# First layer of a four-layer network: twelve pairs of token tiles by seven block products each

## The chip, the cores and the metric

One core of one Trainium2 chip runs the whole program in one launch. The metric is device time in microseconds. TensorE is PE in the profile (its weight loads PEld), VectorE is DVE, ScalarE is ACT, GpSimd is POOL, and SyncE, which here only issues DMAs, is SP.

## The reference, cut to what matters

`x` is 4 x 1024 tokens of 1024 features. The change is in the first of four layers, and in the preparation of the second one's weights, which takes place beside it.

```python
w_masked = L0_attn_weight * elem_mask                    # 1024 x 1024, masked in blocks of 32 x 32
x = layernorm(x + einsum('bsk,nk->bsn', x, w_masked))    # first layer: the whole of it
# second layer, per batch b: weight, bias and a LoRA adapter chosen by b
y = einsum('bsd,od->bso', x, weight) + bias
lo = einsum('bsr,bor->bso', einsum('bsd,brd->bsr', x, A[b]), Bw[b])
x = layernorm(x + y + where(use_lora[b], lo, 0))
# third layer: a sequence model; fourth: a linear layer with routed LoRA experts
```

## The kernel before

The 4096 tokens are 32 tiles of 128, numbered `s` = 0 to 31 in the first layer, 32 to 63 in the second, 64 to 95 in the fourth. Arithmetic is fp32 by splitting: every operand is the sum of a high half (rounded by ACT) and a low half (the rest, by VectorE), and a product of 128 tokens, 128 inputs and 512 outputs is three matmuls, hi by W hi, hi by W lo, lo by W hi (L726 to L728). The identity is added to the weight, so the product already holds `x + x W`. A tile has 8 chunks of inputs (`KC`) and two halves of outputs, 8 x 2 x 3 = 48 matmuls, accumulated in one PSUM bank for each half.

The masked weight `wall_x` is made in the first 43 us: GpSimd multiplies by the mask (L2171), VectorE adds the identity (L1499), ACT takes the high half (L1148), VectorE the low one (L1503). Tiles 0 to 2 run chunk by chunk behind it.

From tile 3 on each tile goes through the same steps. SP loads `x_in` (L504), transposed, into one of two buffers. ACT makes `x_hi` (L1164), VectorE `x_lo` (L1512). TensorE runs `product(s, 0)` and `product(s, 1)`. ACT evacuates each half into `row` (L1169), VectorE takes statistics of each (L1529) and aggregates them (L1534 to L1538), GpSimd takes the root (L2178), ACT makes `shift` (L1176), normalises (L1179) and issues the store (L1182).

Beside tiles 16 to 31 the second layer's weights of batch 0 are made, in 16 parts, one part a tile. SP loads a part (L515); TensorE multiplies the chosen LoRA rows into a bank (`weight_part`, L782); VectorE adds the identity (L1560) and sums bank and part (`weight_sum`, L1562); ACT takes the high half (`weight_hi`, L1236) and VectorE the low one (`weight_lo`, L1568). The rows themselves come from `pick_a` and `pick_b` on TensorE and `take_a`, `take_b` on ACT. In later batches GpSimd makes some of the low halves (L2185).

VectorE also does small tasks once, each beside one tile, in code order: `centre_win` (L1581), `adapter_coef` (L1593), `pick_places`, `mixes`, `take_biases`, `radii`, `first_angle`, nine `angle` (L1656 to L1665), `choose`, `lora_low` (L1626).

Each engine's order in the first layer is plain program order, written out in its own function, and engines meet through counting semaphores. A waiting instruction holds all that is behind it on its engine.

## Time and profile before

| | us |
|---|---|
| median of 3 runs | 1692.5 |
| lowest and highest run | 1691.87, 1694.61 |
| span of the profiled execution | 1690.5 |
| first layer from tile 3 on | about 51 to 376 |

The span is what the trace of one execution covers; the runs are timed from outside and lie about 2 us above it. Busy time of an engine is the sum of what its instructions cover. Matmuls overlap, so that the distance of two starts tells what one costs. In the groups a mean is that of one instruction from start to end. The releaser in brackets is the instruction whose semaphore came last before the idle time ended. The granted clock is the share of TensorE's full clock, of 2.4 GHz, that it was given.

### The profile page before, as it was taken

The numbers are of one execution on the slowest core, as the hardware profiler recorded it, in microseconds if no ns is written. First come the engines' busy times: TensorE is split into PE (matmuls) and PEld (weight loads), VectorE is DVE, ScalarE is ACT, GpSimd is POOL, SyncE is SP. The second block draws the span as 40 slices with busy tenths as digits, with TensorE's granted clock in tenths as the row PEclk, the third lists the DMA queues.
The fourth block names the chain that finished last, engine by engine and source line by source line (L and its number), as shares of the span: only waits on it lengthen the run. The fifth ranks groups of instructions, "written<-read, shape, count | busy, mean of one in ns | idle before, by whom it ended". The sixth has DMA issues, their size and how long they took to land.

```text
span 1690.5 us, 22973 instructions
## 1 busy us (share of the span) xinstructions
PE 1657.1 (98%) x8110; PEld 1341.9 (79%) x8110; DVE 1049.6 (62%) x2004; ACT 648.0 (38%) x939; POOL 434.2 (26%) x371
## 2 busy tenths in 40 slices
PE   8999999999999999999989999999899999999998
PEld 7788888888888888888876666666678788888886
DVE  6444453436555555566777777777967776776633
ACT  3434333433333333322344555555533333433311
POOL 4111111100000000000276777773223221221200
PEclk9999999999999999999999999999999999999999
DMA  7324233333332333332140000002555565555321
GB/s 275 113 100 150 97 116 124 125 112 118 112 110 107 115 113 115 116 138 84 51 171 26 1 1 1 1 1 75 186 179 210 164 204 204 193 190 184 131 88 50
DMA packets 73124, 196.60 MB, mean 116 GB/s; under 512 B 8883, under 2 KB 17075, under 8 KB 72755
## 3 DMA queue, kind: packets, MB, share of 16 engines
q1 hardware_dynamic: 52274, 125.92, 22.3%
q10 hardware_dynamic: 20736, 69.22, 10.2%
q8 instruction: 66, 1.08, 0.3%
q14 instruction: 48, 0.39, 0.1%
HBM read 122.75 MB, written 72.35 MB: 115 GB/s over the span
## 4 chain that ended last, share of the span: by engine, by line
PE 90%; DVE 4%; issue 3%; ACT 1%; POOL 1%; DMA 1%; ACTq 0%; SPq 0%; POOLq 0%; DVEq 0%
PE ps L726 20%; PE ps L728 20%; PE ps L727 20%; PE ps L933 6%; PE ps L875 3%; PE ps L740 3%; PE ps L833 2%; PE ps L881 2%; PE ps L925 2%; PE ps L923 2%; PE ps L924 2%; PE ps L901 1%; PE ps L782 1%; PE ps L847 1%; PE ps L846 1%
## 5 line engine op out<-in xcount | busy, mean ns | idle before, releaser
L726 PE MATMUL ps<-wall_x,x_hi 128*128 128x512 f32 x1008 | 398.8, 396 | 7.6 <-ACT wall_x L1236 3.5
L728 PE MATMUL ps<-wall_x,x_lo 128*128 128x512 f32 x1008 | 393.3, 390 | 0.0
L727 PE MATMUL ps<-wall_x,x_hi 128*128 128x512 f32 x1008 | 393.1, 390 | 0.0
L2178 POOL TENSOR_TENSOR rstd<-var_eps,minus_half 128x1 f32<-128x1 f32 x96 | 78.9, 822 | 882.7 <-DVE minus_mean L1538 882.7
L1529 DVE BATCH_NORM_STATS2 stats<-row 128x6 f32<-128x512 f32 x192 | 133.1, 694 | 175.0 <-ACT row L1169 170.6
L726 PEld LDWEIGHTS ps<-wall_x,x_hi 128*128 128x128 f32 x1008 | 189.5, 188 | 49.4 <-ACT wall_x L1236 5.2
L728 PEld LDWEIGHTS ps<-wall_x,x_lo 128*128 128x128 f32 x1008 | 189.5, 188 | 40.3
L727 PEld LDWEIGHTS ps<-wall_x,x_hi 128*128 128x128 f32 x1008 | 189.8, 188 | 37.2
L726 PE MATMUL ps<-wall_y,x_hi 128*128 128x512 f32 x512 | 202.4, 395 | 0.0
L728 PE MATMUL ps<-wall_y,x_lo 128*128 128x512 f32 x512 | 199.6, 390 | 0.0
L727 PE MATMUL ps<-wall_y,x_hi 128*128 128x512 f32 x512 | 199.4, 389 | 0.0
L1526 DVE TENSOR_TENSOR row<-ps,bias 128x512 f32<-128x512 f32 x128 | 88.0, 687 | 106.2 <-PE ps L728 104.9
L1302 ACT ACTIVATE g<-ps,b 128x512 f32<-128x512 f32 x128 | 83.7, 679 | 122.5 <-PE ps L925 122.0
L933 PE MATMUL ps<-g,w 128*128 128x512 f32 x256 | 125.5, 612 | 0.0
L1164 ACT ACTIVATE x_hi<-ps 128x1024 fp32r<-128x1024 f32 x64 | 65.6, 1025 | 152.2 <-PE ps L740 149.2
L1179 ACT ACTIVATE row<-row,shift,rstd 128x1024 f32<-128x1024 f32 x96 | 119.5, 1244 | 3.2
L728 PEld LDWEIGHTS ps<-wall_y,x_lo 128*128 128x128 f32 x512 | 96.1, 188 | 20.3
L727 PEld LDWEIGHTS ps<-wall_y,x_hi 128*128 128x128 f32 x512 | 96.3, 188 | 19.1
L726 PEld LDWEIGHTS ps<-wall_y,x_hi 128*128 128x128 f32 x512 | 96.2, 188 | 18.7
L1176 ACT ACTIVATE shift<-minus_mean,rstd 128x1 f32<-128x1 f32 x96 | 28.1, 292 | 202.5 <-POOL rstd L2178 202.3
L1562 DVE TENSOR_TENSOR w_first<-ps,w_first 128x512 f32<-128x512 f32 x64 | 44.0, 688 | 87.2 <-PE ps L782 86.7
L1512 DVE TENSOR_TENSOR x_lo<-ps,x_hi 128x1024 fp32r<-128x1024 f32 x64 | 78.0, 1219 | 26.2 <-ACT x_hi L1164 25.9
(282 smaller groups left out, 2827.7 us busy)
## 6 DMA issues: line engine op xcount, KB each, us to landing
x_scratch<-row ACTq DMA_DIRECT2D x64, 512.0 KB, 2.7
x_in<-x_scratch SPq DMA_DIRECT2D x64, 512.0 KB, 3.7
w_first<-in_w_t SPq DMA_DIRECT2D x64, 256.0 KB, 3.0
out<-row ACTq DMA_DIRECT2D x32, 512.0 KB, 2.8
x_in<-in_x_t SPq DMA_DIRECT2D x29, 512.0 KB, 3.4
cx<-x_scratch SPq DMA_DIRECT2D x24, 512.0 KB, 3.9
x_scratch<-cx ACTq DMA_DIRECT2D x24, 512.0 KB, 2.8
w_in<-in_w_t SPq DMA_DIRECT2D x34, 256.0 KB, 3.0
```

What stands on the lines that cost most here:

```text
L726: pe.matmul(bank, hi[:, k], wall[:, k, 0, cols], start=(k == 0), stop=False)
L727: pe.matmul(bank, hi[:, k], wall[:, k, 1, cols], start=False, stop=False)
L728: return pe.matmul(bank, lo[:, k], wall[:, k, 0, cols], start=False, stop=(k == KC - 1))
L740: last = pe.transpose(ps_x[:, k * P:(k + 1) * P], x_in[s % 2][:, k * P:(k + 1) * P], ident[:])
L933: pe.matmul(ps[:, OUT], w2[:, FCH * (n // UNITS) + i], g[:, i], start=(i == 0), stop=(i == FCH - 1)).then_inc(o_done, 1)
L1164: act.activation(flat(x_parts(s)[0]), src, ACT.Identity).then_inc(hi_ready, 1)
L1179: act.activation(row[:, i], row[:, i], ACT.Identity, bias=shift[:, i:i + 1], scale=rstd[:, i:i + 1])\
L1302: act.activation(g[:, i], ps[:, F0 + i % 2], ACT.Silu, bias=of_layer(b1[:, :, i], n))\
L1512: dve.tensor_tensor(lo, src, hi.bitcast(F32), ALU.subtract).then_inc(lo_ready, 1)
L1526: dve.tensor_tensor(row[:, i, cols], ps[:, out_bank(s, half)], bias[:, cols], ALU.add)\
L1529: mark(dve.bn_stats(stats[:, i, half], row[:, i, cols]))
L2178: pool.tensor_tensor(rstd[:, i:i + 1], var_eps[:, i:i + 1], minus_half[:, 0:1], ALU.pow)\
```

## The change

Tiles 5 to 28 are taken in 12 pairs (a, b) = (5, 6), (7, 8), ... A pair is a 2 x 2 block matrix: tile a and tile b by first and last 512 inputs. The weight is 2 x 2 blocks of 512 x 512. The product of the two is made by Strassen's scheme (in Winograd's form) of seven block products in place of eight. The seven left operands are three blocks of the input, A11, A12 (tile a) and A22 (tile b), and four sums of blocks, S1 to S4. The right operands are three blocks of the weight and four sums, T. Each product has 4 chunks x 3 = 12 matmuls, and a pair 84.

- **T** is made once. `t_sums` makes 16 sums of 128x512, in place in the loaded weight, groups 0 and 1 on GpSimd, 2 and 3 on VectorE. `t_hi` on ACT and `t_low` on VectorE split them in eight steps of 128x1024 into `wall_y`, which is free until the second layer's weights.
- **S** is made for every pair by `combine` on GpSimd: four sums of 128x512 into `x_sum`.
- **Splitting**: `op_hi` on ACT and `op_lo` on VectorE, seven each, 128x512.
- **Products**: order A11, A12, S2, S3, S1, S4, A22. A11, S2 and S1 go one on top of the other into bank 0; after each of the three ACT copies the bank into a part of `held` (`hold`), since each partial sum is needed. The other four go into banks 1, 3, 2 and 3, the last on top of the fourth.
- **Joining**: four `join` on VectorE (bank plus held part, into `row`), in place of ACT's four evacuations. Statistics, aggregate, root and normalisation are as before, in another order.
- VectorE's small tasks are in `extra`, called for both tiles of a pair between the low half of S1 and the third join. `split_a` is moved to tile 30, and the buffer `lora_in` holds one half at a time.
- `load_x` of a tile waits for the halves of the pair two tiles back and for the four sums.
- The 16 weight parts are moved beside tiles 29 (6), 30 (5) and 31 (5), with four load buffers in place of two, banks 4 and 6, and the odd low halves on GpSimd. `wall_y` holds T until the last pair's end.
- The semaphore `bias_rows_ready` gives way to a wait of VectorE for its own end, in the last layer.

The core of the diff:

```diff
+S_BEG, S_END = 5, 29
+PAIRS = (S_END - S_BEG) // 2
+PRODUCTS = 7
+A11, A12, S2, S3, S1, S4, A22 = range(PRODUCTS)
+SUM_OF = {S1: 0, S2: 1, S3: 2, S4: 3}
+PLACE_OF = {S2: 0, S3: 1, S4: 2}
+SPREAD_T = ((0, 1), (2, 3), (4, 6), (5, 7))
+GROUPS = 4
+HELD, JOINS, SUMS = 3, 4, 4
+TAIL_PARTS = {S_END: range(0, 6), S_END + 1: range(6, 11), S_END + 2: range(11, PARTS)}
...
+        def op_source(p, j):
+            xa, xb = pair_in(p)
+            if j in SUM_OF:
+                return x_sum[:, SUM_OF[j]]
+            return {A11: xa[:, FIRST_HALF], A12: xa[:, LAST_HALF], A22: xb[:, LAST_HALF]}[j]
+        def op_parts(j):
+            if j in PLACE_OF:
+                return sum_hi[:, PLACE_OF[j]], sum_lo[:, PLACE_OF[j]]
+            slot, first = {A11: (0, 0), A12: (0, GROUPS), S1: (1, 0), A22: (1, GROUPS)}[j]
+            return x_hi[:, slot, first:first + GROUPS], x_lo[:, slot, first:first + GROUPS]
...
+        def op_wall(j, g):
+            if j in (A11, A12, S4):
+                wall, half = wall_x[:, g if j == A11 else GROUPS + g], int(j == S4)
+            else:
+                wall, half = t_place(2 * g + (j in (S2, A22))), int(j in (S2, S3))
+            return [wall[:, i, half * HALF:(half + 1) * HALF] for i in range(2)]
+        def t_sums(eng, semaphore, g, first):
+            b11, b12 = [w0_in[:, g, cols] for cols in (FIRST_HALF, LAST_HALF)]
+            b21, b22 = [w0_in[:, g + GROUPS, cols] for cols in (FIRST_HALF, LAST_HALF)]
+            eng.wait_ge(w0_lo_ready, g + GROUPS + 2)
+            eng.tensor_tensor(b11, b12, b11, ALU.subtract).then_inc(semaphore, 1)
+            eng.tensor_tensor(b12, b22, b12, ALU.subtract).then_inc(semaphore, 1)
+            eng.wait_ge(semaphore, first + 2)
+            eng.tensor_tensor(b22, b22, b11, ALU.subtract).then_inc(semaphore, 1)
+            eng.wait_ge(semaphore, first + 3)
+            eng.tensor_tensor(b21, b21, b22, ALU.subtract).then_inc(semaphore, 1)
...
+                elif paired(s - 2):
+                    p = pair_of(s - 2)
+                    last = A12 if s - 2 == S_BEG + 2 * p else A22
+                    sp.wait_ge(hi_ready, op_count(p, last))
+                    sp.wait_ge(lo_ready, op_count(p, last))
+                    sp.wait_ge(pool_summed, x_sums(p, SUMS - 1))
...
             for s in range(2, A_END):
-                load_x(s + 3)
+                if s != S_END:
...
+                if s == S_END - 2:
+                    for n in range(2):
+                        load_w(n)
+                if s == S_END:
+                    for n in range(2, 6):
+                        load_w(n)
+                    sp.wait_ge(mm_done, product_count(PAIRS - 1, A22))
                     sp.dma_start(a_in[:], a["expert_a"]).then_inc(lora_loaded, 16)
-                if s >= PARTS - 1 and s < 2 * PARTS - 1:
-                    load_w(s - PARTS + 1)
+                    load_x(s + 3)
+                if s > S_END:
+                    for n in TAIL_PARTS[s]:
...
+            def paired_product(p, j):
+                hi, lo = op_parts(j)
+                bank = ps[:, {A11: 0, A12: 1, S2: 0, S3: 3, S1: 0, S4: 2, A22: 3}[j]]
+                pe.wait_ge(hi_ready, op_count(p, j))
+                pe.wait_ge(lo_ready, op_count(p, j))
+                if j == A11:
+                    pe.wait_ge(evac_act, held_count(p - 1, 2) if p > 0 else evac_count(S_BEG - 2, 0))
+                elif j == A12 and p == 0:
+                    pe.wait_ge(evac_act, evac_count(S_BEG - 2, 1))
+                elif j == A12:
+                    pe.wait_ge(evac_dve, join_count(p - 1, 0))
+                elif j == S2:
+                    pe.wait_ge(evac_act, held_count(p, 0))
+                elif j == S3 and p == 0:
+                    pe.wait_ge(evac_act, evac_count(S_BEG - 1, 1))
+                elif j == S3:
+                    pe.wait_ge(evac_dve, join_count(p - 1, 3))
+                elif j == S1:
+                    pe.wait_ge(evac_act, held_count(p, 1))
+                elif j == S4 and p > 0:
+                    pe.wait_ge(evac_dve, join_count(p - 1, 2))
+                elif j == A22:
+                    pe.wait_ge(evac_dve, join_count(p, 1))
+                opens = j not in (S2, S1, A22)
+                for g in range(GROUPS):
+                    if p == 0 and j == S2:
+                        pe.wait_ge(w0_hi_ready, t_count(2 * g + 1))
+                        pe.wait_ge(w0_lo_ready, t_count(2 * g + 1))
+                    w_hi, w_lo = op_wall(j, g)
+                    pe.matmul(bank, hi[:, g], w_hi, start=(opens and g == 0), stop=False, skip_group_check=not opens)
+                    pe.matmul(bank, hi[:, g], w_lo, start=False, stop=False, skip_group_check=not opens)
+                    last = pe.matmul(bank, lo[:, g], w_hi, start=False, stop=(g == GROUPS - 1),
+                                     skip_group_check=not opens)
+                last.then_inc(mm_done, 1)
...
+            for s in range(FIRST, S_BEG):
+                product(s, 0)
+                product(s, 1)
+            for p in range(PAIRS):
+                for j in range(PRODUCTS):
+                    paired_product(p, j)
+                    if p == pair_of(8) and j == S1:
+                        first_biases()
+                    if p == PAIRS - 1 and j in (A12, S3):
+                        pick_b(0, int(j == S3))
+                    if p == PAIRS - 1 and j == S4:
+                        pick_a(0)
+            for s in range(S_END, A_END):
                 if s == A_END - 1:
                     turn_x(A_END)
-                if s >= PARTS and s % 2 == 0:
-                    pick_a((s - PARTS) // 2)
-                product(s, 0)
-                if s == PARTS - 1:
-                    pick_b(0, 0)
-                if s >= PARTS:
-                    weight_part(s - PARTS)
-                product(s, 1)
-                if s == PARTS - 1:
-                    pick_b(0, 1)
-                if s == 8:
-                    first_biases()
+                for i in range(PARTS // 2):
+                    half, k = i // 4, i % 4 * 2
+                    product(s, half, range(k, k + 2))
+                    if i < len(TAIL_PARTS[s]):
+                        n = TAIL_PARTS[s][i]
+                        if n % 2 == 0 and n // 2 + 1 < KC:
+                            pick_a(n // 2 + 1)
+                        weight_part(n)
...
+            def hold(p, i):
+                act.wait_ge(mm_done, product_count(p, (A11, S2, S1)[i]))
+                if p > 0:
+                    act.wait_ge(evac_dve, join_count(p - 1, (0, 3, 2)[i]))
+                act.activation(held[:, i], ps[:, 0], ACT.Identity).then_inc(evac_act, 1)
...
+            for p in range(PAIRS):
+                a, more = S_BEG + 2 * p, p + 1 < PAIRS
+                if p > 0:
+                    op_hi(p, A22)
+                hold(p, 0)
+                if more:
+                    op_hi(p + 1, A11)
+                normalise(a - 1)
+                if more:
+                    op_hi(p + 1, A12)
+                else:
+                    split_x(S_END)
+                hold(p, 1)
+                if more:
+                    op_hi(p + 1, S2)
+                    op_hi(p + 1, S3)
+                else:
+                    take_b(0, 0)
+                hold(p, 2)
+                if more:
+                    op_hi(p + 1, S1)
+                else:
+                    take_b(0, 1)
+                extra(a)
+                extra(a + 1)
+                if more:
+                    op_hi(p + 1, S4)
+                normalise(a)
...
+            def join(p, i):
+                a = S_BEG + 2 * p
+                s, half, bank, part = ((a, 0, 1, 0), (a + 1, 1, 3, 2), (a, 1, 2, 2), (a + 1, 0, 3, 1))[i]
+                cols = slice(half * HALF, (half + 1) * HALF)
+                dve.wait_ge(mm_done, product_count(p, (A12, S3, S4, A22)[i]))
+                dve.wait_ge(evac_act, held_count(p, part))
+                dve.wait_ge(stored[s % 2], 16 * (s // 2))
+                dve.tensor_tensor(row[:, s % 2, cols], ps[:, bank], held[:, part], ALU.add).then_inc(evac_dve, 1)
...
+            for g in range(2, GROUPS):
+                t_sums(dve, summed, g, KC + 1 + SUMS * (g - 2))
+            split_x(FIRST)
+            half_stats(0, 0)
+            half_stats(0, 1)
...
+            for p in range(PAIRS):
+                a, more = S_BEG + 2 * p, p + 1 < PAIRS
+                if p > 0:
+                    join(p - 1, 3)
+                    op_lo(p, A22)
+                    joined_stats(p - 1, 3)
+                    aggregate(a - 1)
+                if more:
+                    op_lo(p + 1, A11)
+                join(p, 0)
+                joined_stats(p, 0)
+                if more:
+                    op_lo(p + 1, A12)
+                    op_lo(p + 1, S2)
+                    op_lo(p + 1, S3)
+                else:
+                    split_x(S_END)
+                join(p, 1)
+                joined_stats(p, 1)
+                if more:
+                    op_lo(p + 1, S1)
+                extra(a)
+                extra(a + 1)
+                join(p, 2)
+                joined_stats(p, 2)
+                aggregate(a)
+                if more:
+                    op_lo(p + 1, S4)
...
+            def combine(p):
+                xa, xb = pair_in(p)
+                for s in range(S_BEG + 2 * p, S_BEG + 2 * p + 2):
+                    pool.wait_ge(x_loaded[s % 2], 16 * x_loads(s))
+                if p > 0:
+                    pool.wait_ge(lo_ready, op_count(p - 1, S1))
+                pool.tensor_tensor(x_sum[:, 0], xb[:, FIRST_HALF], xb[:, LAST_HALF], ALU.add).then_inc(pool_summed, 1)
+                pool.wait_ge(pool_summed, x_sums(p, 0))
+                pool.tensor_tensor(x_sum[:, 1], x_sum[:, 0], xa[:, FIRST_HALF], ALU.subtract).then_inc(pool_summed, 1)
+                pool.tensor_tensor(x_sum[:, 2], xa[:, FIRST_HALF], xb[:, FIRST_HALF], ALU.subtract).then_inc(pool_summed, 1)
+                if p > 0:
+                    pool.wait_ge(lo_ready, op_count(p - 1, S4))
+                pool.wait_ge(pool_summed, x_sums(p, 1))
+                pool.tensor_tensor(x_sum[:, 3], xa[:, LAST_HALF], x_sum[:, 1], ALU.subtract).then_inc(pool_summed, 1)
```

How the instructions stand now on three of the engines. On VectorE at the start, behind the last mask, before: `w0_in` is the masked weight that is loaded, `wall_x` its halves.

```order
L1503 TENSOR_TENSOR wall_x_106<-w0_in_109,wall_x_106 128x1024
L1499 TENSOR_TENSOR w0_in_109<-w0_in_109,ident_51 128x128
L1503 TENSOR_TENSOR wall_x_106<-w0_in_109,wall_x_106 128x1024
L1512 TENSOR_TENSOR x_lo_128<-x_in1_126,x_hi_127 128x1024
L1529 BN_STATS stats_74<-row_129 128x6 x2
```

And after (L542 to L547 are `t_sums`, L1786 is the low half of tile 3):

```order
L1773 TENSOR_TENSOR wall_x_106<-w0_in_109,wall_x_106 128x1024
L1769 TENSOR_TENSOR w0_in_109<-w0_in_109,ident_51 128x128
L1773 TENSOR_TENSOR wall_x_106<-w0_in_109,wall_x_106 128x1024
L542 TENSOR_TENSOR w0_in_109<-w0_in_109 128x512
L543 TENSOR_TENSOR w0_in_109<-w0_in_109 128x512
L545 TENSOR_TENSOR w0_in_109<-w0_in_109 128x512
L547 TENSOR_TENSOR w0_in_109<-w0_in_109 128x512
L542 TENSOR_TENSOR w0_in_109<-w0_in_109 128x512
L543 TENSOR_TENSOR w0_in_109<-w0_in_109 128x512
L545 TENSOR_TENSOR w0_in_109<-w0_in_109 128x512
L547 TENSOR_TENSOR w0_in_109<-w0_in_109 128x512
L1786 TENSOR_TENSOR x_lo_128<-x_in1_126,x_hi_127 128x1024
```

Eight sums have moved in ahead of the low half of tile 3.

On VectorE in the middle of the layer, one tile before, with a small task (`angle`, its first steps) behind the statistics of a half:

```order
L1529 BN_STATS stats_74<-row_129 128x6
L1534 BN_AGGR mean_var_75<-stats_74 128x2
L1537 TENSOR_SCALAR var_eps_76<-mean_var_75 128x1
L1538 TENSOR_SCALAR minus_mean_77<-mean_var_75 128x1
L1512 TENSOR_TENSOR x_lo_128<-x_in1_126,x_hi_127 128x1024
L1529 BN_STATS stats_74<-row_129 128x6
L1560 TENSOR_TENSOR w_first_166<-w_first_166,ident_51 128x128
L1562 TENSOR_TENSOR w_first_166<-ps,w_first_166 128x512
L1568 TENSOR_TENSOR wall_y_107<-w_first_166,wall_y_107 128x512
L1656 TENSOR_TENSOR sq_re_54<-anchor_53 128x4
```

And a piece of a pair after: L1825 is `join`, L1831 statistics, L1810 `op_lo`, L1958 the first step of an angle.

```order
L1825 TENSOR_TENSOR row_129<-ps,held_185 128x512
L1831 BN_STATS stats_74<-row_129 128x6
L1810 TENSOR_TENSOR x_lo_128<-x_in1_126,x_hi_127 128x512
L1810 TENSOR_TENSOR sum_lo_184<-x_sum_182,sum_hi_183 128x512 x2
L1825 TENSOR_TENSOR row_129<-ps,held_185 128x512
L1831 BN_STATS stats_74<-row_129 128x6
L1810 TENSOR_TENSOR x_lo_128<-x_sum_182,x_hi_127 128x512
L1958 TENSOR_TENSOR sq_re_54<-anchor_53 128x4
L1959 TENSOR_TENSOR sq_im_55<-anchor_53 128x4
```

The small task stands between two joins of one pair now, not at a tile's end.

On SP's queue at the end of the layer before, loads of a tile and of a weight part in turn:

```order
L504 DMA x_in0_125<-in_x_t 128x1024
L515 DMA w_first_166<-in_w1_t 128x512
L504 DMA x_in1_126<-in_x_t 128x1024
L515 DMA w_first_166<-in_w1_t 128x512
L495 DMA x_in0_125<-x1_scratch 128x1024
L515 DMA w_first_166<-in_w1_t 128x512
```

And after (L618 loads a tile of the second layer, L642 a weight part, L731 the matrix `a_in` of the last layer's experts):

```order
L642 DMA w_more_167<-in_w1_t 128x512 x2
L642 DMA w_first_166<-in_w1_t 128x512 x2
L731 DMA a_in_154<-in_expert_a 128x1024
L618 DMA x_in0_125<-x1_scratch 128x1024
L618 DMA x_in1_126<-x1_scratch 128x1024
L642 DMA w_more_167<-in_w1_t 128x512 x2
L642 DMA w_first_166<-in_w1_t 128x512 x2
L642 DMA w_more_167<-in_w1_t 128x512
```

The loads of tiles 32 and 33 stand ahead of those of parts 6 to 10.

## Rows read from the trace of the kernel before

**Rows 1.** The page: busy time and instructions of each engine over the span.

```profile
PE 1657.1 (98%) x8110; PEld 1341.9 (79%) x8110; DVE 1049.6 (62%) x2004; ACT 648.0 (38%) x939; POOL 434.2 (26%) x371
```

**Rows 2.** Windows: the first layer from tile 3 on, and a place far behind.

```profile
core 0: us, PE busy (x) PEld busy (x) DVE busy (x) ACT busy (x) POOL busy (x), PEclk, DMA share, GB/s
52.00:376.00 324.00, 322.22 (x1432) 266.44 (x1432) 135.80 (x372) 127.40 (x183) 44.26 (x32) 1.00 0.34 120
...
863.00:867.00 4.00, 1.86 (x11) 1.33 (x11) 4.00 (x3) 0.61 (x1) 2.62 (x2) 1.00 0.55 168
867.00:870.00 3.00, 2.00 (x9) 2.01 (x10) 2.83 (x6) 1.20 (x2) 1.91 (x1) 0.52 0.89 325
```

**Rows 3.** Timeline of TensorE in tile 16: start, duration, line, what.

```profile
195.17 0.39 PE L726 MATMUL ps<-wall_x,x_hi 128*128 128x512 f32 x1
...
199.72 0.39 PE L728 MATMUL ps<-wall_x,x_lo 128*128 128x512 f32 x1
```

**Rows 4.** Timeline of GpSimd and VectorE beside the first tiles; idle time and releaser in brackets.

```profile
29.51 1.92 POOL L2171 TENSOR_TENSOR w_in<-w_in,block_on 128x1024 f32<-128x1024 f32 x1 [1.46 <-DVE block_on L1493]
...
37.58 1.23 DVE L1503 TENSOR_TENSOR wall_x<-w_in,wall_x 128x1024 fp32r<-128x1024 f32 x1
37.61 2.97 POOL L2171 TENSOR_TENSOR w_in<-w_in,block_on 128x1024 f32<-128x1024 f32 x1 [2.44 <-DVE block_on L1493]
...
40.68 0.29 DVE L1499 TENSOR_TENSOR w_in<-w_in,ident 128x128 f32<-128x128 f32 x1 [1.88 <-POOL w_in L2171]
```

**Rows 5.** Groups of instructions from 52 to 376 us: busy, mean ns, idle before.

```profile
L2178 POOL TENSOR_TENSOR rstd<-var_eps,minus_half 128x1 f32<-128x1 f32 x31 | 43.2, 1395 | 275.8 <-DVE minus_mean L1538 275.8
L1529 DVE BATCH_NORM_STATS2 stats<-row 128x6 f32<-128x512 f32 x62 | 42.8, 694 | 170.6 <-ACT row L1169 170.6
L1179 ACT ACTIVATE row<-row,shift,rstd 128x1024 f32<-128x1024 f32 x31 | 38.6, 1244 | 1.0
L1169 ACT ACTIVATE row<-ps 128x512 f32<-128x512 f32 x60 | 35.8, 598 | 118.7 <-PE ps L728 113.2 <-DMA x_scratch<-row 2.7 <-ACT row L1179 2.7
...
L1568 DVE TENSOR_TENSOR wall_y<-w_first,wall_y 128x512 fp32r<-128x512 f32 x16 | 11.1, 692 | 11.2 <-ACT wall_y L1236 11.2
L1562 DVE TENSOR_TENSOR w_first<-ps,w_first 128x512 f32<-128x512 f32 x16 | 10.9, 683 | 0.3
L1236 ACT ACTIVATE wall_y<-w_first 128x512 fp32r<-128x512 f32 x16 | 10.1, 632 | 24.2 <-DVE w_first L1562 24.2
...
L1534 DVE BATCH_NORM_AGGREGATE mean_var<-stats 128x2 f32<-128x12 f32 x31 | 6.5, 209 | 1.1
...
L1626 DVE SCALAR_TENSOR_TENSOR lora<-lora_in,low_row,lora 128x1024 fp32r<-128x1024 f32 x2 | 2.5, 1268 | 0.0
```

**Rows 6.** Groups of GpSimd over the whole span.

```profile
L2178 POOL TENSOR_TENSOR rstd<-var_eps,minus_half 128x1 f32<-128x1 f32 x96 | 78.9, 822 | 882.7 <-DVE minus_mean L1538 882.7
...
L2185 POOL TENSOR_TENSOR wall_x<-w_more,wall_x 128x512 fp32r<-128x512 f32 x8 | 10.3, 1292 | 23.0 <-ACT wall_x L1236 23.0
```

**Rows 7.** Timeline: TensorE at tiles 3 and 4, and the issue of a store.

```profile
50.87 0.44 PE L726 MATMUL ps<-wall_x,x_hi 128*128 128x512 f32 x1
...
59.50 0.33 ACTq L1182 DMA_DIRECT2D x_scratch<-row  x1
...
62.98 0.47 PE L726 MATMUL ps<-wall_x,x_hi 128*128 128x512 f32 x1 [1.01 <-issue]
```

**Rows 8.** Timeline of VectorE: first step of the adapter coefficients; one angle, first and last.

```profile
91.78 0.29 DVE L1593 TENSOR_REDUCE group<-ident 128x3 f32<-128x48 f32 x2
...
203.69 0.15 DVE L1656 TENSOR_TENSOR sq_re<-anchor 128x4 f32<-128x4 f32 x1
...
204.97 0.16 DVE L1665 TENSOR_TENSOR anchor<-anchor,fix 128x4 f32<-128x4 f32 x1
```

**Rows 9.** The page's DMA issues: count, size, median us from issue to landing.

```profile
w_first<-in_w_t SPq DMA_DIRECT2D x64, 256.0 KB, 3.0
...
x_in<-in_x_t SPq DMA_DIRECT2D x29, 512.0 KB, 3.4
```

398 lines of the change are left out of this document (283 added, 115 removed).

## The prediction

> **What bounds the kernel now.** I read the busy table first: TensorE is busy 98% of the span, VectorE 62%, GpSimd 26% [rows 1]. Then the windows: in the whole stretch that the change rewrites, 52 to 376 us, TensorE is busy 322.2 of 324 us at a granted clock of 1.00, with VectorE at 136 us and GpSimd at 44 [rows 2]. So the first layer is bound by the number of matmuls alone; what the other engines do there is hidden, and their time counts only where the new order makes TensorE wait for it. The price of a matmul is its spacing, not its duration: from the one at 195.17 to the twentieth after it at 199.72 are 4.55 us, 0.2275 us each (both are listed as 0.39, since they overlap) [rows 3].
>
> **What is saved.** A pair of tiles took 2 x 48 = 96 matmuls and takes 7 x 12 = 84; 12 pairs save 144. 144 x 0.2275 = **-32.8 us**. The 16 products for the next weights and the picks are moved, not removed. All further terms are waits that TensorE gets in exchange. One product of twelve lasts 2.73 us, a pair 19.1.
>
> **What is added at the start.** Sixteen 128x512 sums of first-layer weights (T) stand on GpSimd (8) and on VectorE (8), the latter ahead of tile 3's low half. GpSimd and VectorE disturb each other there today: GpSimd's mask takes 1.92 us, but 2.97 when it starts just behind VectorE's 1024-wide subtraction of 1.23 us [rows 4], so that subtraction keeps the other out for 2.97 - 1.92 = 1.05 us, 0.18 less than it is listed with. A 128x512 operation on two SBUF operands is listed with 1.29 us on GpSimd and 0.69 on VectorE [rows 5, 6]; I take 1.07 to 1.1 and 0.55 for what each holds. The last mask ends at 37.61 + 2.97 = 40.58. Today VectorE's next step starts right then [rows 4]; now GpSimd goes straight on with its first sum to 41.9. VectorE's last identity ends at 42.1, its last low half falls behind GpSimd's third sum and ends at 45.5; then the five GpSimd sums that are left and the first five of VectorE alternate, 5 x (1.07 + 0.55) = 8.1, to 53.6; VectorE's other three, each of which needs the one before, take 2.1, to 55.7; the low half of tile 3 takes 1.2 and ends at 56.9. TensorE began tile 3 at 50.87 [rows 7]: +6.1. The 1.0 to 1.2 us that it waits today ahead of tile 4, for that tile's low half (to 62.98), goes, as ACT and VectorE are then ahead: **+4.9** (between 2, if the two engines do not exclude each other for these shapes, and 9, if every sum is stretched as the mask was).
>
> The Trainium skill ("SBUF — State Buffer", section on the two separate sides) has the rule behind this: GpSimd and a VectorE operation with two SBUF inputs take a shared pair of ports for a whole instruction each, while one that reads PSUM with one SBUF operand is outside the rule. The trace agrees: GpSimd's root takes 1.40 us on average in the first layer, where low halves read two SBUF operands, and (78.9 - 43.2) / 65 = 0.55 in the later layers, where they read PSUM [rows 5, 6]. By the rule the new joins (PSUM plus held) cost nothing beside GpSimd; without it they would add up to 4 x 0.5 us to a pair.
>
> **The first wait inside the pairs.** TensorE's third product of a pair goes to the bank of its first and so waits until ACT has copied that one into held. For pair 0 that copy stands far back in ACT's row. Let T be the end of tile 4's last matmul. The first four halves of pair 0 need the buffers of tile 3, and ACT and VectorE, kept busy by T, reach them late; only behind their four low halves, by my count at T+0.5, does VectorE take the second statistics of tile 3. These and the aggregate take it to T+1.6, GpSimd's root to T+3.2, shift and normalise on ACT to T+4.8. Then ACT issues the store (0.45), evacuates (0.5), makes two 1024-wide high halves of T (2.0), evacuates (0.5), makes three high halves (1.6) and copies (0.6) [rows 5, 7]: T+10.4. TensorE is there after two products, T+5.5: **+4.9** (3 to 8).
>
> **The pairs' own circle.** A tile's buffer is loaded again only when both halves of the pair's last operand and the four sums have been read. Around that circle, TensorE apart: landing 3.4 [rows 9]; three dependent GpSimd sums, 3 x 1.29 plus 0.35 of exclusion, 4.2; high half 0.6 and low half 0.7 with 0.8 of exclusion, 2.1; join, statistics, low half of S1, 2.0; next join, statistics, aggregate, 1.85; root 1.0, shift 0.3, normalise 1.24, store issue 0.45, 3.0; high and low half of A22, 1.3 [rows 5, 6]. With 0.35 for handovers this is 18.2 us, against 19.1 of TensorE: a margin of only 0.9 us. But VectorE's other work of the first layer (`extra`) stands inside this circle, between the low half of S1 and the join after S4, where today it lies in VectorE's idle time. By pair: centring 2.8 (two 1024-wide steps and two small ones) and adapter coefficients 1.9 (from 91.78 on) = 4.7; places and mixes 2.2; bias, low half of the window and nine small ones 2.5; eleven small ones 1.6; two angles (203.69 to 205.13 = 1.44 each), one LoRA half 1.27 and a choice 0.3 = 4.5; two angles 2.9; two and a LoRA half 4.2; two 2.9; one 1.4 [rows 5, 8]. Together 26.9, estimates where no row stands (small ones at 0.15). What exceeds the margin in these nine pairs is 26.9 - 9 x 0.9 = **+18.8**; pairs 9 to 11 have none. The bounds are 6 and 27: circle 2.6 us shorter than TensorE's pair, or as long.
>
> The joins, the held copies and the seven halves of a pair otherwise fit: ACT has 7 x 0.63 + 3 x 0.6 + 2 x 1.99 = 10.2 us of 19.1, VectorE about 11.5 and GpSimd about 7.5. If the circle above were not there, these would cost nothing.
>
> **The tail.** All 16 weight parts are now beside tiles 29 to 31, 6, 5 and 5, every 1.4 us of matmuls, where they were one per 11 us. The first pick waits for ACT about 0.9. Parts 6 to 10 are queued on SP behind the load for tile 33, which waits for the low half of tile 31, that is for the end of tile 29 plus 2.3 us; with two issues (0.8), landing 3.5, identity 0.3 and sum 0.7 part 6 is summed about 8 us after tile 29's end, and TensorE needs it for part 8 after 4.8: +3.4 [rows 5, 9]. A chunk of A behind the normalisation of tile 29 on ACT costs 2.2, one of 0.5, and the last choice, now after the sums, 1.3. Sum **+8.5** (3 to 12, the bounds being only the queue, and all of it with slower landings). The later load of tile 33 itself is hidden by the 20 us that follow.
>
> **The clock.** Around 865 TensorE is busy 1.86 of 4 us, and the next 3 us are granted 0.52 [rows 2], the 1.2 GHz level. The new waits of 4 to 6 us at the start could do the same; most of what runs slowly there is followed by another wait, which takes it up. **+1.5** (0 to 8).
>
> **Sum.** -32.8 + 4.9 + 4.9 + 18.8 + 8.5 + 1.5 = +5.8 on the profiled 1690.5, a span of 1696.3. The median of the runs, 1692.5, lies 2.0 above that span, so 1698.3; I say **1698**. A measurement tells 0.2%, 3.4 us: faster is below 1689.1, slower above 1695.9.
>
> **Rivals.**
> 1. Near: the circle lasts 17.5, not 18.2, with 3.0 us for a landing as the weights have [rows 9] and no exclusion. The margin is 1.6; the extras' excess is 12.7, the tail 7, the clock 0.5: -32.8 + 9.8 + 12.7 + 7 + 0.5 = -2.8, 1689.7 (this case reaches to 1693). For it: landings of 3.0 are common in the page. Against: each sum on GpSimd meets two-operand work on VectorE.
> 2. Clearly faster (other side): the circle lasts at most 16.5, because handovers and roots cost what they do undisturbed (0.55). The extras' excess falls to 6.2, start and pair 0 to 6 together, tail 5, clock nothing: -15.6, **1677**. The point that decides is a circle of 17.5 us, a margin of 1.6: there the excess is 12.7, about the 32.8 - 9.8 - 8.5 - 1.5 = 13.0 that start and tail leave of the saving. Against it are the exclusions of [rows 4].
> 3. Dearer: exclusion and landings at full price. The circle is as long as TensorE's pair, extras cost 27, start 12, tail 11, clock 5: +22, **1714.5**.
> 4. The change does not do what it says, for instance since waits of its own keep the pairs in the old time: 1692.5.
>
> **How the numbers follow.** Forecast case (1693 to 1704) 0.46, near 0.25, clearly faster 0.17, dearer 0.10, no effect 0.02. Slower by over 0.2%: 0.40 of the forecast case and 0.10 of the dearer one, 0.50. Within 0.2%: 0.06 + 0.18 + 0.02 = 0.26. Faster: 0.17 + 0.07 = 0.24. The range 1683 to 1709 leaves out most of 2 and 3, 0.2 in all.
>
> **What would show it.** In the changed profile: 144 matmuls fewer; tile 3 of TensorE starting near 57; about 5 us of idle TensorE ahead of the first S2, released by ACT's held; in pairs 0 to 8 idle time ahead of S2 of about extras less 0.9 (3.8 in pair 0, 0.5 in pair 8) and none in pairs 9 to 11; 3.4 us ahead of part 8; the granted clock below 1 after the start's waits. The prediction is wrong if pairs with extras run at 19.1 us (then rival 2), if also pairs without them take more (then rival 3, the circle alone is too long), or if the wait is named for a row's join or a load instead of the held copy.

## The result, and the profile after

| | us |
|---|---|
| median of 4 runs of the changed kernel | 1704.7 |
| lowest and highest | 1703.9, 1708.7 |
| median of 4 runs of the kernel before, same chip | 1693.4 |
| ratio of the runs | 1.0071, 95% interval 1.0059 to 1.0083 |
| profiled span after (before 1690.5) | 1703.5 |

The changed kernel is slower by 11.3 us, 0.7%. The forecast was 1698, slower by 5.5, with a range to 1709. The busy table of the changed kernel's page:

```profile
PE 1642.0 (96%) x7966; PEld 1321.5 (78%) x7966; DVE 1147.5 (67%) x2120; ACT 672.3 (39%) x995; POOL 517.8 (30%) x435
```

Against [rows 1] TensorE has 144 matmuls fewer, VectorE 98 us more to do and GpSimd 84. Where the time went is seen at one landmark, ACT's normalisation of tile 31, the last of the first layer. The timeline of ACT, before (first fence) and after:

```profile
380.30 1.24 ACT L1179 ACTIVATE row<-row,shift,rstd 128x1024 f32<-128x1024 f32 x1
...
852.13 1.24 ACT L1179 ACTIVATE row<-row,shift,rstd 128x1024 f32<-128x1024 f32 x1
```

```profile
391.64 1.24 ACT L1402 ACTIVATE row<-row,shift,rstd 128x1024 f32<-128x1024 f32 x1
...
865.37 1.24 ACT L1402 ACTIVATE row<-row,shift,rstd 128x1024 f32<-128x1024 f32 x1
```

The first layer ends 11.3 us later; the second rows, of the second layer's last tile, are 13.2 apart, so that 1.9 more came in the second layer, which the change leaves alone; later layers add nothing. The windows of the changed kernel (columns as in [rows 2]): the first layer, two pieces of it, and the piece of the second layer that lost the 1.9.

```profile
52.00:386.00 334.00, 303.39 (x1284) 244.05 (x1284) 229.70 (x486) 149.05 (x237) 114.13 (x88) 0.97 0.32 117
57.50:61.50 4.00, 4.00 (x10) 3.11 (x10) 3.86 (x11) 1.53 (x2) 1.89 (x2) 0.50 0.61 202
113.50:116.50 3.00, 3.00 (x8) 2.32 (x7) 2.46 (x7) 1.23 (x2) 1.09 (x2) 0.50 0.53 175
...
775.50:779.00 3.50, 3.50 (x10) 2.71 (x9) 1.93 (x3) 1.54 (x2) 0.07 (x1) 0.51 0.42 164
```

Where [rows 2] had 1.8 us of idle TensorE in 324, there are 30.6 in 334, and stretches at a granted clock of 0.50, the 1.2 GHz level. Three more of them are at 199, 243 and 359 us. The waits themselves, in TensorE's timeline (idle time and releaser in brackets): tile 3, the first S2, those of pairs 1 and 5, weight part 8.

```profile
56.71 0.77 PE L865 MATMUL ps<-wall_x,x_hi 128*128 128x512 f32 x1 [6.15 <-issue]
...
88.42 0.47 PE L946 MATMUL ps<-wall_y,sum_hi 128*128 128x512 f32 x1 [1.68 <-ACT x_hi L1370]
...
112.94 0.47 PE L946 MATMUL ps<-wall_y,sum_hi 128*128 128x512 f32 x1 [3.72 <-ACT held L1377]
...
198.17 0.47 PE L946 MATMUL ps<-wall_y,sum_hi 128*128 128x512 f32 x1 [3.09 <-ACT held L1377]
...
359.57 0.77 PE L962 MATMUL ps<-b_rows,a_rows 128*128 128x512 f32 x1 [4.26 <-DVE w_more L1864]
```

The profile puts the first S2 down to a high half that ran beside ACT's copy; the copy itself ended at 88.21, 0.2 us before S2 starts.

At the start the sums of T are held off as forecast. Timeline of GpSimd and VectorE there:

```profile
46.67 1.74 POOL L542 TENSOR_TENSOR w_in<-w_in 128x512 f32<-128x512 f32 x1
48.37 1.74 POOL L543 TENSOR_TENSOR w_in<-w_in 128x512 f32<-128x512 f32 x1
...
47.29 1.67 DVE L545 TENSOR_TENSOR w_in<-w_in 128x512 f32<-128x512 f32 x1
48.99 1.67 DVE L547 TENSOR_TENSOR w_in<-w_in 128x512 f32<-128x512 f32 x1
...
54.05 0.69 DVE L545 TENSOR_TENSOR w_in<-w_in 128x512 f32<-128x512 f32 x1
55.39 1.22 DVE L1786 TENSOR_TENSOR x_lo<-x_in,x_hi 128x1024 fp32r<-128x1024 f32 x1
```

Each engine starts a sum every 1.7 us while the other works too; with GpSimd done, VectorE's takes 0.69. Tile 3's low half ends at 56.6, and TensorE goes on.

Below, a wait is the distance of two matmul starts less the usual 0.2275. By that measure the waits ahead of S2 in pairs 1 to 9 are 3.9, 0.3, 1.7, 1.0, 3.3, 1.2, 3.2, 1.2 and 0.4, together 16.1. S2 of pair p + 1 stands behind the small tasks that are called in pair p.

### The profile page after: what moved, and what is told of

Its sections match the earlier page's. It is cut to its first block, busy times and chain, and to the rows that moved or that the text cites. A ratio compares the mean times of both kernels' runs of the same rounds, so it can differ in the third digit from the quotient of the medians.

```text
span 1703.5 us, 23156 instructions
## 1 busy us (share of the span) xinstructions
PE 1642.0 (96%) x7966; PEld 1321.5 (78%) x7966; DVE 1147.5 (67%) x2120; ACT 672.3 (39%) x995; POOL 517.8 (30%) x435
## 4 chain that ended last, share of the span: by engine, by line
PE 76%; DVE 9%; issue 5%; ACT 4%; POOL 3%; DMA 2%; ACTq 0%; SPq 0%; POOLq 0%; DVEq 0%
PE ps L865 13%; PE ps L867 13%; PE ps L866 13%; PE ps L1113 6%; PE ps L1055 3%; PE ps L879 3%; PE ps L946 2%; PE ps L948 2%; PE ps L947 2%; PE ps L1061 2%; PE ps L1013 2%; PE ps L1104 2%; PE ps L1105 2%; PE ps L1103 2%; ACT row L1402 1%
## 5 line engine op out<-in xcount | busy, mean ns | idle before, releaser
L2558 POOL TENSOR_TENSOR rstd<-var_eps,minus_half 128x1 f32<-128x1 f32 x96 | 66.4, 692 | 761.4 <-DVE minus_mean L1840 748.7
L865 PE MATMUL ps<-wall_x,x_hi 128*128 128x512 f32 x624 | 251.1, 402 | 12.8 <-issue 6.1
L867 PE MATMUL ps<-wall_x,x_lo 128*128 128x512 f32 x624 | 245.9, 394 | 0.0
L866 PE MATMUL ps<-wall_x,x_hi 128*128 128x512 f32 x624 | 245.7, 394 | 0.0
L865 PEld LDWEIGHTS ps<-wall_x,x_hi 128*128 128x128 f32 x624 | 118.8, 190 | 40.0 <-issue 10.2
L867 PEld LDWEIGHTS ps<-wall_x,x_lo 128*128 128x128 f32 x624 | 118.6, 190 | 25.7
L866 PEld LDWEIGHTS ps<-wall_x,x_hi 128*128 128x128 f32 x624 | 119.0, 191 | 23.1
L1803 DVE BATCH_NORM_STATS2 stats<-row 128x6 f32<-128x512 f32 x144 | 99.8, 694 | 17.3 <-ACT row L1392 12.9
L866 PEld LDWEIGHTS ps<-wall_y,x_hi 128*128 128x128 f32 x512 | 96.2, 188 | 19.1
L1864 DVE TENSOR_TENSOR w_first<-ps,w_first 128x512 f32<-128x512 f32 x56 | 38.5, 689 | 88.3 <-PE ps L962 87.5
L1786 DVE TENSOR_TENSOR x_lo<-ps,x_hi 128x1024 fp32r<-128x1024 f32 x64 | 78.0, 1219 | 27.0 <-ACT x_hi L1356 26.6
```

Of the source, the lines that this page charges most:

```text
L865: pe.matmul(bank, hi[:, k], wall[:, k, 0, cols], start=(k == 0), stop=False)
L866: pe.matmul(bank, hi[:, k], wall[:, k, 1, cols], start=False, stop=False)
L867: return pe.matmul(bank, lo[:, k], wall[:, k, 0, cols], start=False, stop=(k == KC - 1))
L1786: dve.tensor_tensor(lo, src, hi.bitcast(F32), ALU.subtract).then_inc(lo_ready, 1)
L1803: mark(dve.bn_stats(stats[:, i, half], row[:, i, cols]))
L2558: pool.tensor_tensor(rstd[:, i:i + 1], var_eps[:, i:i + 1], minus_half[:, 0:1], ALU.pow)\
```

## The experiments

All ran beside the kernel before on their own chip (medians 1692.9 to 1693.2). Each edits the changed kernel; times are to be held against its 1704.7.

**e1: the small tasks behind the chain.** On VectorE, and on ACT:

```diff
                 if more:
                     op_lo(p + 1, S1)
-                extra(a)
-                extra(a + 1)
                 join(p, 2)
                 joined_stats(p, 2)
                 aggregate(a)
                 if more:
                     op_lo(p + 1, S4)
+                extra(a)
+                extra(a + 1)
...
-                extra(a)
-                extra(a + 1)
                 if more:
                     op_hi(p + 1, S4)
                 normalise(a)
+                extra(a)
+                extra(a + 1)
```

> Change undone in one part only: VectorE's small tasks (extra) come after the aggregate and the low half of S4, so behind the chain that leads to the held copy (ACT's part of extra moves behind the pair's last normalisation). Theory (the small tasks delay join, aggregate, root, normalisation and so the held copy, on which S2 waits, and the waits of over 3 us drop the clock for 3.4 us each): the waits ahead of S2 in pairs 1 to 9, 16 us in the changed kernel, fall to under 3, and the three slow stretches at 113, 199 and 243 us go: 1704.7 - 13 - 5 = 1687. Rival 1 (the pair's circle itself is too long, VectorE late wherever the tasks stand): 1702 to 1705. Rival 2 (the slow clock costs nothing, as another wait takes it up): 1691 to 1692.

Measured 1689.7, ratio to before 0.9977 (0.9967 to 0.9988). Of TensorE's groups from 92 to 300 us, the one with the most idle time ahead of it, in the changed kernel (one more, `x_hi`, has 1.2) and in e1:

```profile
L946 PE MATMUL ps<-wall_y,sum_hi 128*128 128x512 f32 x75 | 31.8, 424 | 14.6 <-ACT held L1377 14.5
```

```profile
L946 PE MATMUL ps<-wall_y,x_hi 128*128 128x512 f32 x88 | 35.1, 399 | 4.2 <-ACT held L1377 4.2
```

S2 (`sum_hi`) waits no more; S1 (`x_hi` by T), which needs the second copy, waits 4.7 in three pairs. The first layer ends 16.8 us sooner. Rival 1 falls. The three slow stretches in the pairs were to go, and there are still four in all, at 54, 88, 194 and 341 us, with as much slow time as in the changed kernel. The time lies between the theory's 1687 and rival 2's 1691. So the gain is of waits, and the clock's part is not told by this run.

**e2: VectorE's sums behind the low halves.**

```diff
-            for g in range(2, GROUPS):
-                t_sums(dve, summed, g, KC + 1 + SUMS * (g - 2))
             split_x(FIRST)
             half_stats(0, 0)
             half_stats(0, 1)
             aggregate(0)
+            t_sums(dve, summed, 2, KC + 1)
             split_x(FIRST + 1)
+            t_sums(dve, summed, 3, KC + 1 + SUMS)
```

> VectorE's eight sums for T come behind the low halves of tile 3 (four) and tile 4 (four) in place of ahead of tile 3's. Theory (ACT's list before pair 0 is what ends last): tile 3 starts near 51.5 in place of 56.7, and the slow stretch at 55 to 62 us goes, but the held copy of pair 0 comes no more than 1 us sooner, so that the wait ahead of the first S2 grows from 1.8 to 6 or more: 1703 to 1704. Rival (start and pair 0 add up, as the prediction summed them): 5.2 of wait and 3.4 of slow clock less, 1696.

Measured 1705.8, 1.0073 (1.0055 to 1.0091). Tile 3 starts at 51.3, and the time comes back ahead of pair 0's first and third product:

```profile
76.28 0.47 PE L946 MATMUL ps<-wall_x,x_hi 128*128 128x512 f32 x1 [2.97 <-DVE x_lo L1810]
...
87.98 0.76 PE L946 MATMUL ps<-wall_y,sum_hi 128*128 128x512 f32 x1 [4.38 <-ACT x_hi L1370]
```

The two terms of the start are not independent: what is spared at tile 3 is waited for at pair 0.

**e3: tile 33's load behind those of parts 6 to 10.**

```diff
-                if s != S_END:
+                if s != S_END and s != S_END + 1:
                     load_x(s + 3)
...
                 if s > S_END:
                     for n in TAIL_PARTS[s]:
                         load_w(n)
+                if s == S_END + 1:
+                    load_x(s + 3)
```

> The load of tile 33 is queued on SP behind the loads of weight parts 6 to 10, not ahead. Theory (those loads stand behind one that waits for tile 31's low half): the wait of 4.25 us ahead of part 8's product goes, and with it the slow stretch at 359 to 362.5 us (1.7): 1699. Rival (the next wait, for a chunk of A, takes its place): 1703 to 1705.

Measured 1699.7, 1.0043 (1.0024 to 1.0063): 5 us, as the theory had it. Part 8 no longer waits; the wait for a chunk of A behind it grows only from 1.0 to 1.7. Groups of TensorE from 336 to 392 us, changed kernel and e3:

```profile
L962 PE MATMUL ps<-b_rows,a_rows 128*128 128x512 f32 x16 | 7.0, 440 | 5.4 <-DVE w_more L1864 5.4
```

```profile
L964 PE MATMUL ps<-b_rows,a_rows 128*128 128x512 f32 x17 | 7.1, 418 | 1.1 <-DVE w_more L1866 1.1
```

**e4: the three together,** and on ACT before pair 0:

```diff
             t_hi(5)
-            normalise(3)
             evacuate(4, 0)
             t_hi(6)
             t_hi(7)
             evacuate(4, 1)
+            normalise(3)
```

> The three together, and on ACT tile 3's normalisation behind both evacuations of tile 4 in place of ahead of the first. Theory (all terms of the sum but about 3.5 us at pair 0 and 5 in the tail are waits that the order makes; nearly no slow stretches in the first layer): 32.8 saved, some 15 us of waits left, 1.7 of clock: 1675 to 1678. Rival (waits replace each other, the pairs are bound by VectorE and GpSimd): 1688 or more.

Measured 1682.1, 0.9928 (0.9910 to 0.9946). Faster than both, 4 us above the upper end of the expectation: the first layer ends 12.2 us before that of the kernel before, with some 18 us of waits and 3.2 of slow matmuls, and 3.5 are given back in the second layer at a slow stretch near 750.

**e5: the waits filled with small matmuls,** so that the clock stays up.

```diff
                 for j in range(PRODUCTS):
+                    keep_busy(7, {(1, 2): 15, (5, 2): 12, (7, 2): 12, (0, 2): 6, (3, 2): 5, (2, 2): 0, (6, 2): 3, (8, 2): 3}.get((p, j), 0))
                     paired_product(p, j)
...
             for s in range(FIRST, S_BEG):
+                if s == FIRST:
+                    keep_busy(7, 25)
                 product(s, 0)
...
+                        keep_busy(5, {8: 14}.get(n, 0))
                         weight_part(n)
```

> The changed kernel with small matmuls put on TensorE, into a bank that nobody reads, ahead of the products that it waits for (25 ahead of tile 3, 15 ahead of pair 1's S2, 12 at pairs 5 and 7, 14 at weight part 8, a few at others), each stretch of them shorter than the wait that it fills. Theory (the slow clock behind a long wait is a cost of its own, about 7.8 us of slow matmuls in the first layer): no slow stretch there, no product started later, 1704.7 - 7 = 1698, somewhat less if the next wait grows. Rival (the slow matmuls are paid out of later waits): the waits left grow by as much, 1703 to 1705.

Measured 1704.4, 1.0067 (1.0053 to 1.0081): the rival. The same windows as above are at full clock:

```profile
57.50:61.50 4.00, 4.00 (x19) 3.30 (x19) 3.90 (x10) 1.54 (x2) 2.27 (x2) 1.00 0.67 214
113.50:116.50 3.00, 3.00 (x15) 2.47 (x14) 2.29 (x6) 1.43 (x2) 1.16 (x2) 1.00 0.55 175
```

Slow matmuls, counted as what their distances have above 0.2275 us, cost 3.3 us in place of 8.9, and yet the first layer ends only 0.1 sooner. The 2.6 us of the stretch at 55 had been taken out of pair 0's wait: S2 now waits 3.1 behind its filler and 4.6 with it, not 1.8. The same holds in part for the pairs: filler and wait ahead of S2 in pairs 1 to 9 are 18.1 us here, where the waits were 16.1. The three slow stretches in the pairs, 4.8 us, give 2.2 back; the normalisation of tile 28 stands 2.4 sooner, 0.2 of it from the start. The tail, where a chunk of A then waits 3.1 in place of 1.0 and the clock falls behind that wait, gives these away again.

**e6: GpSimd's sums of T on 4 columns.**

```diff
             for g in range(2):
-                t_sums(pool, pool_summed, g, SUMS * g)
+                pool.wait_ge(w0_lo_ready, g + GROUPS + 2)
+                for i in range(SUMS):
+                    w = w0_in[:, g + GROUPS * (i // 2), HALF * (i % 2):HALF * (i % 2) + 4]
+                    at_least(pool, pool_summed, SUMS * g + i)
+                    pool.tensor_tensor(w, w, w, ALU.add).then_inc(pool_summed, 1)
```

> GpSimd's eight sums for T are made on 4 columns in place of 512, so groups 0 and 1 of T are left out; VectorE still makes its eight ahead of tile 3's low half. Theory (VectorE is held off by GpSimd, not busy: its sums are listed with 1.7 us beside GpSimd's, 0.69 alone): all eight take 0.7 us each, tile 3 starts within 1 us of the kernel before (51 in place of 56.7) and pair 0 keeps its own wait ahead of S2 of about 5: 5 us and the slow stretch at 55 us less, 1697 to 1699. Rival (eight sums on VectorE cost their own time): tile 3 near 56 still, 1703 to 1705.

The kernel leaves out half of T, so its results are not those of the network; it is there for its time. Measured 1699.0, 1.0044 (1.0029 to 1.0060); the profiled execution took 1704.0. On VectorE:

```profile
42.80 0.68 DVE L542 TENSOR_TENSOR w_in<-w_in 128x512 f32<-128x512 f32 x1
...
47.50 0.69 DVE L547 TENSOR_TENSOR w_in<-w_in 128x512 f32<-128x512 f32 x1
49.06 1.23 DVE L1786 TENSOR_TENSOR x_lo<-x_in,x_hi 128x1024 fp32r<-128x1024 f32 x1 [0.87 <-ACT x_hi L1356]
```

All eight fit into the time that VectorE idles away before tile 3's high half. Tile 3 starts at 50.42, with no wait. So the 6.3 us at tile 3 are the exclusion, not the work. Pair 0's wait is 4.8 here.

**e7: the input sums on 4 columns,** from the second pair on:

```diff
+                n = HALF if p == 0 else 4
+                FH, LH = slice(0, n), slice(HALF, HALF + n)
...
-                pool.tensor_tensor(x_sum[:, 0], xb[:, FIRST_HALF], xb[:, LAST_HALF], ALU.add).then_inc(pool_summed, 1)
+                pool.tensor_tensor(x_sum[:, 0, 0:n], xb[:, FH], xb[:, LH], ALU.add).then_inc(pool_summed, 1)
```

> GpSimd's four input sums of each pair but the first are made on 4 columns in place of 512, so most of S is left out; all waits stay. Theory of the prediction (the circle load, sums, halves, joins, root, normalisation, A22, load is 18.2 us, of which sums and exclusion are some 5): a margin of 5 us or more, so that the extras hardly show, S2 waits of 16 fall to 3: 1704.7 - 13 - 5 = 1687. Rival (what S2 waits for is the chain from the end of S4's matmuls over join, statistics, aggregate, root, normalisation and A22's high half to the held copy, behind the small tasks; GpSimd's sums are beside it): the waits fall by about a quarter to a half only, 1696 to 1700.

This kernel too leaves out what the network needs, most of S. Measured 1700.4, 1.0047 (1.0032 to 1.0062): the rival again. The run shows that the prediction's circle is not all that holds S2.

```profile
L946 PE MATMUL ps<-wall_y,sum_hi 128*128 128x512 f32 x81 | 33.6, 415 | 10.5 <-ACT held L1377 10.3
```

With GpSimd's sums gone, S2 still waits 3.0, 0.3, 0.8, 0.3, 2.6, 1.2, 2.4, 1.2, nothing: 11.8 of 16.1. What else holds S2? The chain of waits of the changed kernel around the wait of 1.2 us at 220 (pair 6), from S1's last matmul to S2's first; its rows are start, length and what ran:

```profile
208.00 0.24 PE ps L948
208.26 0.61 ACT held L1377
...
208.95 0.70 DVE row L1825
...
210.28 0.67 DVE x_lo L1810
210.96 0.07 DVE sq_re L1958
...
213.64 0.17 DVE anchor L1967
213.83 0.70 DVE row L1825
214.55 0.70 DVE stats L1831
...
215.60 0.15 DVE minus_mean L1840
215.76 1.00 POOL rstd L2558
...
216.84 0.30 ACT shift L1399
...
217.17 1.25 ACT row L1402
218.44 0.33 ACTq L1405
...
219.41 0.59 ACT held L1377
220.00 0.14 issue
220.13 0.47 PE ps L946
```

The join behind S3 needs two things: S3's bank and the held copy of **S1's** product (`part` 2 in `join(p, 1)`). So it cannot run before S1 is done and copied, at 208.95, and everything behind it on VectorE follows: low half of S1, two angles, next join, statistics, then GpSimd, ACT, and the copy. From 208.24 to 220.13 are 11.9 us, of which the angles are 2.9 and the rest 9.0. TensorE has four products in between, 10.9. By this path the wait is what the small tasks exceed 1.9, and with e7's waits this holds in the other pairs too: the extras of 4.7, 4.5, 4.2 and 2.9 leave 2.8, 2.6, 2.3 and 1.0, where 3.0, 2.6, 2.4 and 1.2 were measured.

The changed kernel waits longer than that in six pairs, and there the circle ended last. On VectorE the join stands behind the low half of S3 too, which comes from the load over GpSimd's sums. Timeline ahead of pair 5's wait:

```profile
184.08 1.55 DVE L1810 TENSOR_TENSOR sum_lo<-x_sum,sum_hi 128x512 fp32r<-128x512 f32 x1
184.24 0.60 ACT L1377 ACTIVATE held<-ps 128x512 f32<-128x512 f32 x1 [0.19 <-PE ps L948]
185.55 0.68 DVE L1825 TENSOR_TENSOR row<-ps,held 128x512 f32<-128x512 f32 x1
```

The copy is there at 184.84, the low half 0.8 us later, and the join goes right behind it. Ahead of the waits of pairs 1, 3, 4, 5, 7 and 9 the low half is later than the copy by 0.8 to 1.1 us; ahead of those of pairs 2, 6 and 8 the copy is later. e7 takes 0.3 to 0.9 us off just those six waits and nothing off the other three. So two paths of nearly the same length lead to S2, both through the small tasks, and shortening one gains no more than the lead that it has: 4.3 of 16.1 us.

**e8: e4 with its waits filled,** and one low half of T ahead of tile 3's statistics.

```diff
+                    keep_busy(7, {(0, 0): 10, (0, 2): 12, (1, 4): 3, (5, 4): 9}.get((p, j), 0))
                     paired_product(p, j)
...
                 op_lo(0, j)
+            t_low(5)
             half_stats(3, 1)
             aggregate(3)
-            t_low(5)
```

> The four edits of e4_all, one 1024-wide low half of T ahead of tile 3's second statistics, and small matmuls ahead of pair 0's first and third product and of S1 in pairs 1 and 5, where 1 to 4 us are waited. Theory: as e4_all, less the two slow stretches in the first layer (3.2 us): 1682.1 - 3 = 1679. Rival (the second layer's and third layer's slow stretches, which have shown at other places in every variant, decide the rest): between 1676 and 1684 whatever the first layer does.

Measured 1679.3, 0.9918 (0.9904 to 0.9932). The intervals of e4 and e8 overlap, so the two are not told apart by their runs; in the profiles the first layer has no slow stretch from tile 3 on and ends 2.0 sooner than e4's.

**e9: one normalisation behind the copy,** a test of the chain just shown.

```diff
                 hold(p, 0)
+                if p > 0:
+                    normalise(a - 2)
                 if more:
                     op_hi(p + 1, A11)
                 normalise(a - 1)
...
                 if more:
                     op_hi(p + 1, S4)
-                normalise(a)
+                else:
+                    normalise(a)
```

> One move in the changed kernel: on ACT the normalisation of a pair's first tile, and the issue of its store, come behind the next pair's copy for S2, not ahead of it; VectorE's small tasks stay where they are. Corrected theory (S2 waits for a chain that runs through TensorE: end of S1's product, held, join, statistics, low half, the small tasks, join, statistics, aggregate, root, shift, normalise, store issue, held; 9.2 us and the small tasks against 10.9 us of TensorE): root, shift, normalise and issue, 3.2 us of it, no longer stand ahead of the copy, so the waits ahead of S2 in pairs 1 to 9 (16.0 us in the changed kernel) fall below 2, with their slow stretches: 1704.7 - 14 - 2 = 1688 to 1690. Rival 1 (the circle over the loads, as predicted): the store and so the next load come later, no gain, 1703 to 1706. Rival 2 (joins then wait for the store, whose issue is now later): half of it, 1696.

Measured 1688.3, 0.9966 (0.9956 to 0.9977), inside what the corrected chain gave, and outside both rivals' numbers. From 92 to 300 us:

```profile
L946 PE MATMUL ps<-wall_y,x_hi 128*128 128x512 f32 x88 | 34.8, 396 | 1.7 <-DVE row L1828 1.0 <-ACT held L1377 0.6
```

The small tasks stand where they stood, and S2 does not wait. The run does not tell the two paths apart: in this order the normalisation stands no longer ahead of A22's high half either, for which the next load waits, so the circle is shorter by it too. Rival 1 had the next load wait for the store; in `load_x` it waits for the halves and the sums.

**e10 and e11: e9 with the other edits.** e10 is e9 with those of e3 and e2, of e4 on ACT before pair 0 and of e8 on VectorE. e11 adds fillers:

```diff
+                    keep_busy(7, {(0, 0): 10, (0, 2): 12, (1, 4): 3}.get((p, j), 0))
                     paired_product(p, j)
```

> e9 with the load of tile 33 behind parts 6 to 10, VectorE's sums for T behind the low halves of tiles 3 and 4, and before pair 0 tile 3's normalisation and statistics moved back. Theory: e9's gain, 5 of the tail, 3 at pair 0: 1688 - 9 = 1679, less up to 3 if the late normalisation also spares the waits ahead of S1 that moving the small tasks left (4.7 us): 1675. Rival: as e4 and e8, 1679 to 1682, the small tasks' place making no difference.

> e10 with small matmuls on TensorE ahead of A11 and S2 of pair 0 and S1 of pair 1. Theory (a slow stretch behind a wait is paid for in part, as e5 showed 0.7 of 1.7 us in the pairs): 0.7 to 1.7 us less than e10. Rival: no difference, within 0.5 us.

Measured e10 1677.8, 0.9905 (0.9889 to 0.9922), e11 1676.2, 0.9904 (0.9887 to 0.9920): 15 and 17 us faster than the kernel before, and 27 and 28 faster than the changed one. e10's first layer ends at 362.25 by the landmark above, 18.1 before that of the kernel before. The fillers make no difference that can be measured.

## Why the prediction came out as it did

It was right in its sign and its range: the saving of 144 matmuls is more than eaten by waits of the new order. Its sum was +5.8 where the first layer measured +11.3: the waits were forecast 4.0 too high, and the clock and the first matmuls behind waits 10 too low. Term by term, in us:

| term | forecast | measured |
|---|---|---|
| 144 matmuls | -32.8 | 144 fewer; without waits a pair takes 19.1 (pairs 10, 11) |
| start | +4.9 | 6.3 at tile 3, less 1.0 ahead of tile 4: +5.3 |
| pair 0 | +4.9 | 1.8 at S2, 1.4 at A22: +3.2 |
| S2 behind the small tasks | +18.8 | +16.1 |
| tail | +8.5 | 0.9, 4.3, 1.0, 1.3, 1.1: +8.5 |
| clock, first layer | +1.5 | 8.9 of slow matmuls: 2.6 at the start, 1.6 in each of three pairs, 1.5 in the tail |
| first matmuls behind waits | none | +2.6 |
| ahead of tile 3 | none | -0.5: the last matmul there starts at 50.17, before at 50.64 |

- **The start** held with its mechanism. The tile was forecast at 57.0 and stood at 56.7; e6 shows that the exclusion is the whole of it. What failed is the independence of this term: e2 shows that it can't be saved by itself, since ACT and VectorE reach pair 0 late either way.
- **Pair 0**: 3.2 is the term mis-sized by the clock. The slow matmuls of tile 3 brought TensorE later to S2; in e5 and e6, without them, S2 waits 4.6 (filler and rest) and 4.8 us, near the 4.9 of the forecast.
- **The circle** was read rightly, but it is only one of two paths. Where it ended last it has the forecast length, seen in SP's timeline as the distance from the load of one pair's second tile to the next pair's:

```profile
175.78 0.33 SPq L627 DMA_DIRECT2D x_in<-in_x_t  x1
198.33 0.33 SPq L627 DMA_DIRECT2D x_in<-in_x_t  x1
...
284.44 0.33 SPq L627 DMA_DIRECT2D x_in<-in_x_t  x1
302.64 0.33 SPq L627 DMA_DIRECT2D x_in<-in_x_t  x1
```

The first two are 22.55 us apart with 4.5 of small tasks between, the last two 18.2 with none; the forecast was 18.2 plus the small tasks. What failed is the prediction's next step, that if the circle were not there the joins, copies and halves "would cost nothing": e7 shortens the circle by its sums, and 11.8 us of waits stay. The path from S1's copy, which `join(p, 1)` needs, has 9.0 us and the small tasks against 10.9 of TensorE, and the prediction did not have it. That 18.8 came near 16.1 owes something to luck, since this second path happens to be shorter by only about 1 us. With filler in place of the slow stretches the same waits are 18.1 (e5), so the slow matmuls had taken some of them up.
- **The tail** held in its sum (its terms as listed come to 8.3, not 8.5). The piece behind SP's queue was 4.3 (forecast 3.4), shown by e3; the chunk behind the normalisation cost 1.0 (2.2) and a late sum 1.3 (0.5).
- **The clock** was mis-sized: five slow stretches, also behind the waits of 3.2 to 4.3 us in the pairs and the tail, where the forecast thought of those at the start; 8.9 us of slow matmuls. But the step's reasoning, that another wait takes much of it up, is what e5 showed. Of 4.8 slow us in the pairs 2.2 were paid, of 2.6 at the start nearly none.
- **Behind a wait** the first distance of two matmuls is 0.08 to 0.1 us above 0.2275, and with many waits of under 0.1 us each this comes to 2.6 us more than before. The prediction had no such term.
- **The second layer's 1.9** was not foreseen, see below. The runs, 11.3 apart where the profiles are 13.0, say that it isn't the same in every run.

Rival 1 and rival 2 put the decision at a circle of 17.5 us; e7 takes the sums out of it, forecast at 4.2 of its 18.2 us, and gained only 4.3 us in the runs. Rival 3's full price of exclusion and landings did not show: pairs without small tasks have no wait.

## What to carry to other kernels

Where a product waits for a copy, write down for each operand of each join which product it comes from, and follow the path from each of them, not only the longest: a second path right behind the first one caps what shortening the first can gain. Small work put in front of a join that both share is paid for beyond their margin. Put what nobody waits for, here a normalisation and its store, behind the copy that frees a bank. A saving on the bounding engine is worth having only once its new partners are in an order that leaves it no wait: the same seven products gave +11 us in one order and -16 in another.
